# Expert layer of a decoder kernel: fp16 products from two scaled parts, and its sums spread over three engines

## The reference, cut to what matters

```python
x = x + self_attention_0(layernorm(x))
x = x + cross_attention_0(layernorm(x), ctx)
x = x + experts(layernorm(x))            # the part that changes
x = x + linear_attention_1(layernorm(x))
x = x + cross_attention_1(layernorm(x), ctx)
x = x + quantised_ffn(layernorm(x))

def experts(x, gate_w, weight):          # gate_w 8 x 256, weight 8 x 256 x 256
    logits = einsum('bsd,ed->bse', x, gate_w)
    topk_vals, topk_idx = top_k(logits, 2)
    topk_weights = softmax(topk_vals)
    one_hot = one_hot(topk_idx, 8)
    weights_full = einsum('bsk,bske->bse', topk_weights, one_hot)
    expert_out = einsum('bsd,edh->bseh', x, weight)
    return einsum('bse,bseh->bsh', weights_full, expert_out)
```

## Time and profile before

| what | us |
|---|---|
| median of 3 runs (2026.10 to 2026.39) | 2026.26 |
| the profiled execution | 2026.75 |
| its span | 2025.0 |
| TensorE busy (share of the span) | 1762.7 (87%) |
| VectorE busy | 1612.1 (80%) |
| ScalarE busy | 1334.7 (66%) |
| GpSimd busy | 274.6 (14%) |

### The profile page before, as it was taken

The page is one execution under the profiler, slowest core; times in us unless marked ns, Lnnn a source line. Parts: engine busy times, 40 slices in busy tenths (PEclk is TensorE's granted clock), DMA queues, the critical chain, the costliest instruction groups (busy, mean ns, idle before and its releaser), DMA issues. The chain is left out here.

```text
span 2025.0 us, 39718 instructions
## 1 busy us (share of the span) xinstructions
PE 1762.7 (87%) x14926; PEld 707.2 (35%) x14926; DVE 1612.1 (80%) x2323; ACT 1334.7 (66%) x2530; POOL 274.6 (14%) x534
## 2 busy tenths in 40 slices
PE   7757989999999999989999999997799775589962
PEld 3421222322332232223222222222444443367641
DVE  3789999989999999878999999990677676566656
ACT  3325989889889989978999999997210443234341
POOL 0810111211111021111101010100200132000003
PEclk9967999999999999989999999999899988699985
DMA  4000000000000001000000000000100000000001
GB/s 122 0 0 1 2 1 1 2 1 2 2 1 2 1 1 51 2 1 2 1 1 2 1 2 1 2 2 30 56 0 0 1 0 0 0 1 1 1 1 42
DMA packets 11147, 17.38 MB, mean 9 GB/s; under 512 B 1857, under 2 KB 9025, under 8 KB 10721
## 3 DMA queue, kind: packets, MB, share of 16 engines
q1 hardware_dynamic: 10128, 13.64, 2.1%
q10 hardware_dynamic: 848, 1.38, 0.2%
HBM read 12.92 MB, written 2.10 MB: 7 GB/s over the span
## 5 line engine op out<-in xcount | busy, mean ns | idle before, releaser
L968 DVE TENSOR_REDUCE mxp<-ps_m 128x2 f32<-128x1024 f32 (+1 forms) x960 | 1089.5, 1187 | 92.6 <-PE ps_m L779 91.0
L903 ACT ACTIVATE work<-ps_s 128x512 f32<-128x512 f32 x1856 | 1010.5, 598 | 135.1 <-PE ps_s L792 86.3
L806 PE MATMUL ps_av<-work,vst 128*32 128x256 f32 x7424 | 595.9, 393 | 11.9 <-ACT avs L910 11.2
L779 PE MATMUL ps_m<-k_stack,qa 48*128 48x512 f16 (+1 forms) x2048 | 380.2, 369 | 24.1 <-DVE mxp L968 23.5
L792 PE MATMUL ps_s<-qb,k_stack 50*128 50x512 f16 x1856 | 365.8, 383 | 31.0 <-ACT work L903 24.9
L806 PEld LDWEIGHTS ps_av<-work,vst 128*32 128x32 f32 x7424 | 147.4, 108 | 347.6 <-ACT work L903 259.5
L792 PEld LDWEIGHTS ps_s<-qb,k_stack 50*128 50x128 f16 x1856 | 109.5, 93 | 424.7 <-ACT work L903 408.6
L779 PEld LDWEIGHTS ps_m<-k_stack,qa 48*128 48x128 f16 x2048 | 105.5, 95 | 66.7 <-DVE mxp L968 56.3
L1175 PE MATMUL mprodp<-w_experts,mxt 128*128 128x512 f32 x256 | 117.2, 602 | 0.0
L198 PE MATMUL prod<-w_qkv,xt 128*128 128x512 f32 (+1 forms) x256 | 93.2, 508 | 7.1 <-DVE k_rows L1100 6.7
L1247 DVE SCALAR_TENSOR_TENSOR x_res<-mprodp,mmix,x_res 128x256 f32 (+1 forms) x128 | 61.7, 482 | 31.0 <-PE mprodp L1175 30.5
(11 more groups left out here) (309 smaller groups left out, 1783.9 us busy)
## 6 DMA issues: line engine op xcount, KB each, us to landing
x_res<-in_x SPq DMA_DIRECT2D x4, 512.0 KB, 13.6
w_experts<-in_w_experts SPq DMA_DIRECT2D x1, 2048.0 KB, 7.9
out<-x_res SPq DMA_DIRECT2D x8, 256.0 KB, 2.1
ctx_c<-in_ctx_c SPq DMA_DIRECT2D x1, 1664.0 KB, 8.4
work<-in_ctx_t SPq DMA_DIRECT2D x1, 784.0 KB, 11.2
w_qkv<-in_w_qkv ACTq DMA_DIRECT2D x1, 768.0 KB, 11.1
w_qkv<-in_w_qkv SPq DMA_DIRECT2D x1, 768.0 KB, 4.0
work<-in_ctx_t SPq DMA_DIRECT2D x1, 672.0 KB, 6.7
```

The source lines that it names most:

```text
L779: m = pe.matmul(ps_m[:, b, e, col:col + width], qa[n % 3][e * HALF:e * HALF + MAXROWS, j, a, :], STACKS[g][e * HALF:e * HALF + MAXROWS, gr ...
L806: m = pe.matmul(ps_av[32 * h:32 * h + 32, cols], vst[n % 2][:, t, h, :], pbuf[(tau[n] + t) % 2][:, h, cols], start=(t == 0 and half == 0), ...
L903: a.activation(pbuf[g % 2][:, h, :], ps_s[:, b, :], ACT.Exp, scale=factor).then_inc(s["exp"], 1)
L968: v.tensor_reduce(dst, src, AX.X, ALU.max).then_inc(s["mred"], 1)
```

## The change

What it does:

- **Weights.** The experts' weights, scaled by a power of two, are split into a high and a low fp16 part (`weh`, `wel`, together 32 KB of a partition, in the memory of the layer's first key stack, which now lives on). VectorE does it in the last attention unit: the peak at step 0, the rest behind two small products of TensorE at steps 5 and 7 that bring the peak to all partitions.
- **Rows.** A tile's turned rows times 64 are split too: ScalarE writes the high part `xh`, VectorE the low part `xl`. The float32 copy `xt` stays, for the gate. The gate's weights are divided by the scales (`gain`).
- **Products.** Each bank is six fp16 multiplications, high times high, high times low, low times high, in place of two in float32. The banks are filled in the order 3, 2, 0, 1.
- **Sums.** Bank 3, and bank 2 of the odd tiles, are weighed by ScalarE into SBUF (`scaled`), and GpSimd adds those parts to `x` after VectorE has added its own: two additions for even tiles, four for odd ones, each behind the last. VectorE is left with six or four. The statistics of a tile wait for GpSimd and stand one tile later on VectorE.
- **Fetch.** The normalising of the rows goes from VectorE to GpSimd.
- The loop is written out for all 16 tiles.

```diff
+ROW_GAIN = 64.0
...
+                    if expert_peak_at(n, t):
+                        pe.wait_ge(s["kpeak"], 4)
+                        b = take_m()
+                        pe.transpose(ps_m[0:1, b, 0, 0:P], wpeak[:, :], ident[:, :]).then_inc(s["mx"], 1)
+                    if expert_spread_at(n, t):
+                        pe.wait_ge(s["mred"], expert_peak_done)
+                        b = take_m()
+                        pe.matmul(ps_m[:, b, 0, 0:1], ones[0:1, :], wtop[:, :], start=True, stop=True).then_inc(s["mx"], 1)
...
+                    if (n, t) == (NCH - 1, 0):
+                        v.wait_ge(s["late"], 16 * len(later))
+                        v.tensor_reduce(wpeak[:, :], we[:, :, :], AX.XY, ALU.max, apply_absolute_value=True).then_inc(s["kpeak"], 1)
+                    if expert_peak_at(n, t):
+                        b = take()
+                        v.tensor_reduce(wtop[:, :], ps_m[0:1, b, 0, 0:P], AX.X, ALU.max).then_inc(s["mred"], 1)
+                    if expert_spread_at(n, t):
+                        b = take()
+                        v.tensor_copy(wbound[:, :], ps_m[:, b, 0, 0:1]).then_inc(s["mred"], 1)
+                        v.wait_ge(s["mred"], taken[0])
+                        cw = Counted(v, s["wchain"])
+                        power_scale(v, cw, wbound[:, :], wfloor[:, :], wscale[:, :], wback[:, :])
+                        cw(v.tensor_scalar(gain[:, :], wscale[:, :], ROW_GAIN, None, ALU.mult))
+                        cw(v.tensor_scalar(weh[:, :, :], we[:, :, :], wscale[:, :], None, ALU.mult))
+                        cw.wait()
+                        cw(v.scalar_tensor_tensor(wel[:, :, :], we[:, :, :], wscale[:, :], weh[:, :, :], ALU.mult, ALU.subtract))
+                        cw.wait()
...
-def experts(prog, x, st, mean, rstd, gate, w, iota, ident):
+def experts(prog, x, st, mean, rstd, gate, weh, wel, gain, iota, ident):
...
+    ORDER = (3, 2, 0, 1)
...
+    def by_act(n):
+        return (3,) if n % 2 == 0 else (3, 2)
+    def by_dve(n):
+        return [b for b in ORDER if b not in by_act(n)]
+    def more_until(n):
+        return sum(2 * len(by_act(m)) for m in range(n))
...
+        xh, xl = ([sb(f"mx{k}{p}", [P, 2, P], F16) for p in range(2)] for k in "hl")
+        scaled = [sb(f"mscaled{p}", [P, 4, D]) for p in range(2)]
...
+        @block.gpsimd
+        def _(g):
+            def fetch(n):
+                if n >= 2:
+                    g.wait_ge(s["turned"], n - 1)
+                g.tensor_scalar(xn[n % 2][:, :], x[:, n, :], mean[:, n:n + 1], rstd[:, n:n + 1], ALU.subtract, ALU.mult)\
+                 .then_inc(s["fetch"], 1)
+            fetch(0)
+            fetch(1)
+            for n in range(T):
+                if n + 2 < T:
+                    fetch(n + 2)
+                g.wait_ge(s_free[by_act(n)[-1]], n + 1)
+                g.wait_ge(s_free[by_dve(n)[-1]], n + 1)
+                done = more_until(n)
+                for i in range(2 * len(by_act(n))):
+                    if i > 0:
+                        g.wait_ge(s["more"], done)
+                    g.tensor_tensor(x[:, n, :], x[:, n, :], scaled[n % 2][:, i, :], ALU.add).then_inc(s["more"], 1)
+                    done += 1
...
+            def turn_tile(n):
+                pe.wait_ge(s["fetch"], n + 1)
+                if n >= 2:
+                    pe.wait_ge(s["low"], n - 1)
...
-            def multiply(n, p):
-                if has(n + 1):
-                    turn_tile(n + 1, 1 - p)
-                for b in range(4):
-                    if b == 1 and has(n + 1):
-                        logits(n + 1, 1 - p)
-                    s_used.wait(pe, 4 * n + b - 3)
-                    for k in range(2):
-                        m = pe.matmul(prod[:, b, :], xt[p][:, k, :], w[:, k, b * 512:b * 512 + 512],
-                                      start=(k == 0), stop=(k == 1))
-                    m.then_inc(s_w.sem, 1)
-            s_gate.open(pe)
...
+            def products(n, b):
+                if n >= 1:
+                    pe.wait_ge(s_free[b], n)
+                cols = slice(b * 512, b * 512 + 512)
+                for k in range(2):
+                    pe.matmul(prod[:, b, :], xh[n % 2][:, k, :], weh[:, k, cols], start=(k == 0), stop=False)
+                    pe.matmul(prod[:, b, :], xh[n % 2][:, k, :], wel[:, k, cols], start=False, stop=False)
+                for k in range(2):
+                    m = pe.matmul(prod[:, b, :], xl[n % 2][:, k, :], weh[:, k, cols], start=False, stop=(k == 1))
+                m.then_inc(s_prod[b], 1)
+            turn_tile(0)
+            logits(0)
+            for n in range(T):
+                if n + 1 < T:
+                    turn_tile(n + 1)
+                pe.wait_ge(s["low"], n + 1)
+                products(n, ORDER[0])
+                if n + 1 < T:
+                    logits(n + 1)
+                for b in ORDER[1:]:
+                    products(n, b)
...
-            def copy(n, p):
-                s_w.wait(a, 4 * (n - 1))
-                a.wait_ge(s_turned, n + 1)
-                a.copy(xt[p][:, :, :], turn[p][:, 0:D].rearrange("p (k n) -> p k n", k=2)).then_inc(s_copied.sem, 1)
-                a.wait_ge(s_d, n + 1)
-                a.activation(ex[:, :], dif[:, :], ACT.Exp).then_inc(s_e, 1)
...
+            def prepare(n):
+                a.wait_ge(s["turned"], n + 1)
+                if n >= 2:
+                    a.wait_ge(s["gate"], n - 1)
+                src = turn[n % 2][:, 0:D].rearrange("p (k n) -> p k n", k=2)
+                a.copy(xt[n % 2][:, :, :], src).then_inc(s["copied"], 1)
+                if n >= 2:
+                    a.wait_ge(s_prod[ORDER[-1]], n - 1)
+                a.activation(xh[n % 2][:, :, :], src, ACT.Copy, scale=ROW_GAIN).then_inc(s["high"], 1)
+            def exponent(n):
+                a.wait_ge(s["dif"], n + 1)
+                a.activation(ex[:, :], dif[:, :], ACT.Exp).then_inc(s["exp"], 1)
+            def weigh(n, i):
+                b = by_act(n)[i]
+                a.wait_ge(s["mix"], (n + 1) * per)
+                if n >= 2:
+                    a.wait_ge(s["more"], more_until(n - 1))
+                a.wait_ge(s_prod[b], n + 1)
+                for h in range(2):
+                    e = 2 * b + h
+                    m = a.activation(scaled[n % 2][:, 2 * i + h, :], half(b, h), ACT.Copy, scale=mix[n % 2][:, e:e + 1])
+                m.then_inc(s_free[b], 1)
+            prepare(0)
+            exponent(0)
+            for n in range(T):
+                if n + 1 < T:
+                    prepare(n + 1)
+                weigh(n, 0)
+                if n + 1 < T:
+                    exponent(n + 1)
+                if len(by_act(n)) > 1:
+                    weigh(n, 1)
...
+            def low(n):
+                v.wait_ge(s["high"], n + 1)
+                if n >= 2:
+                    v.wait_ge(s_prod[ORDER[-1]], n - 1)
+                v.scalar_tensor_tensor(xl[n % 2][:, :, :], turn[n % 2][:, 0:D].rearrange("p (k n) -> p k n", k=2), ROW_GAIN,
+                                       xh[n % 2][:, :, :], ALU.mult, ALU.subtract).then_inc(s["low"], 1)
+            def statistics(n):
+                v.wait_ge(s["more"], more_until(n + 1))
+                v.bn_stats(st[:, n, :], x[:, n, :]).then_inc(s["st"], 1)
...
+                v.wait_ge(s["exp"], n + 1)
+                c(v.tensor_scalar(den[:, :], ex[:, :], 1.0, gain[:, :], ALU.add, ALU.mult))
...
-            def body(n, p):
-                if has(n + 2):
-                    v.wait_ge(s_turned, n + 1)
-                    fetch(v, xn[p], n + 2).then_inc(s_fetch, 1)
...
+            def accumulate(n):
+                we = mix[n % 2]
+                c = Counted(v, s["sum"], sum(len(by_dve(m)) for m in range(n)))
+                for b in by_dve(n):
+                    v.wait_ge(s_prod[b], n + 1)
+                    c(v.scalar_tensor_tensor(x[:, n, :], half(b, 0), we[:, 2 * b:2 * b + 1], x[:, n, :], ALU.mult, ALU.add))
+                    yield
+                    c.wait()
+                    v.scalar_tensor_tensor(x[:, n, :], half(b, 1), we[:, 2 * b + 1:2 * b + 2], x[:, n, :], ALU.mult, ALU.add)\
+                     .then_inc(s_free[b], 1)
+                    yield
+                    v.wait_ge(s_free[b], n + 1)
+            low(0)
+            for _ in mixture(0):
+                pass
+            for n in range(T):
+                if n + 1 < T:
+                    low(n + 1)
+                turns = [accumulate(n)] + ([mixture(n + 1)] if n + 1 < T else [])
                 while turns:
                     turns = [g for g in turns if next(g, "done") != "done"]
-            for n in range(2):
-                fetch(v, xn[n], n).then_inc(s_fetch, 1)
-            list(mixture(0, 0))
-            every(body, v)
+                if n >= 1:
+                    statistics(n - 1)
+            statistics(T - 1)
...
+        ks = sb(ctx, "k_stack", [P, H // 2, S], F16)
```

(2 more changed lines are left out.)

109 lines of the change are left out of this document (40 added, 69 removed).

## The result

| kernel | median us | lowest to highest | runs |
|---|---|---|---|
| before | 2026.33 | 2026.10 to 2026.39 | 4 |
| changed | 2006.88 | 2006.14 to 2007.64 | 4 |

By the medians the changed kernel takes 19.5 us less, 0.9904 of the time before; the ratio estimated from all fast runs is 0.9898, 95% interval 0.9885 to 0.9912. The forecast was 2010. The median lies at the lower end of the range of 2006 to 2019, 0.9 us inside it; by the ratio the time is 2005.7, 0.3 us under it. The profiled execution took 2007.64 us.

What follows compares the result with a forecast made beforehand. TensorE's float32 product columns were taken to bound the expert stage; fp16 products with two late chains cut it from 126.1 to 109.6 us, 16.5 less, minus 0.3 for small matmuls: 16.2 less, about 2010 us, range 2006 to 2019.

Steps and rivals of the forecast that it cites:

- TensorE's bare tile: Expert stage: 5.20 us of fp16 products plus 0.66 of transposes and logits, 5.86 us a tile without waits.
- ScalarE's chain: Exponential, two bank 2 weighings, then copy: TensorE waits 0.7 us for the copy before every second tile's logits.
- E: The end of the odd tile's last product on TensorE, from which the times within a pair are counted.
- GpSimd's chain: Four additions of 0.83 us from E + 1.87, then a 1.22 us fetch, handed over at E + 6.46.
- GpSimd's slowness: Rival: beside busy VectorE, an add takes 1.05 us and a fetch 1.6; 2021 us, half of it 2015.5; chance 0.22.
- The pair: Odd tile and the even one behind it in the expert stage: 12.5 us in place of 15.08, eight times.
- Start and end of the stage: Expert stage's edges: 5.5 us as before, plus 0.8 for the first fetch and 3.3 for the last adds.
- The split: Attention's last unit: VectorE's weight split, high and low part 4.5 us each, done at 1405.5, covered with 4 us spare.
- Outside the stage: Two small TensorE matmuls in the attention's last unit were to cost 0.3 us.
- The likeliest case: The forecast itself: a pair between 12.2 and 12.9 us, 2007.5 to 2013.5 us; chance 0.60.
- rival C: TensorE's clock drops to 1.2 GHz in the stage through its new waits; 2052 us if half the products; chance 0.04.
- rival B: Both new waits vanish, a pair takes 2 x 5.86 = 11.7 us, 6 us less, 2004 us; chance 0.08.

Runs made afterwards that it cites:

- one_bank: Changed kernel with ScalarE weighing one bank in every tile instead of two in odd ones: 2000.26 us; repeated beside the changed kernel, 2000.23 us.
- weigh_first: Changed kernel with ScalarE weighing bank 2 of an odd tile before the next tile's exponential instead of behind it: 2002.80 us.
- early_fetch: Changed kernel with GpSimd's normalising fetch issued one tile earlier, ahead of a tile's additions instead of behind them: 2008.35 us.
- no_adds: Changed kernel with each GpSimd addition replaced by a copy of one column, so the output lacks what ScalarE weighed: 2006.66 us.
- weigh_early: Changed kernel with ScalarE weighing both banks before the exponential and GpSimd fetching three tiles ahead: 2003.38 us.
- split_thrice: Changed kernel with the high and low part of the weights computed three times in the same place: 2014.36 us.
- fp16_vector: Changed kernel's fp16 products, but all eight sums and the fetch on VectorE, nothing weighed by ScalarE, GpSimd idle: 1999.06 us; repeated, 2000.32 us.

## Why the prediction was right in kind, and which terms were off

The mechanism came as forecast: TensorE's products, now in fp16, bound the tile, and every second tile has a new wait for ScalarE's copy. What failed are sizes in the sum, all to the same side: the 5.86 us of TensorE's bare tile, which measured 5.76 (1.6 us in 16 tiles); the charge of this wait to eight pairs, while it occurs seven times (0.8 us); and the 0.3 us outside the stage, where the span gained 0.7.

**Products: right.** TensorE bounds the stage before, and its columns were the gain. 24 products of 0.217 apart were taken from another stage; the stage's own are 0.215 apart on average (six from 1506.68 to 1507.97 in the even tile of the timeline).

**TensorE's bare tile: 0.1 us too long.** I kept 0.66 us of the earlier trace rows for transposes and logits, worked out from a tile of float32 records. The trace of after has 5.76 where I had 5.86: 24 x 0.215 = 5.16 and 0.60. Over 16 tiles this is 1.6 us, the largest error of the sum.

**ScalarE's chain: right in kind, and placed to 0.1 us.** The exponential was to start at E + 0.77 and starts at E + 0.82; the copy was to be there at E + 2.13, and TensorE takes it at E + 2.07; the wait was to be 0.7 and is shown as 0.56, counted from the modelled end of the last product. Counted as the prediction counts it, from when TensorE could issue (in a tile without the wait the logits start 0.22 us behind the last product before them, which here would be 1505.49), it is 0.72. The next transposes come at E + 6.42, where I had TensorE ready at E + 6.42 and the fetch's handover at E + 6.46. That this chain, with the second bank in it, holds the pair, one_bank shows, and weigh_first for the most part of it.

**GpSimd's chain: its place right, its weight not.** The additions start at E + 1.84 (E + 1.87), take 3.21 (3.32), and the fetch lands at E + 6.26 (E + 6.41). I called both chains equal, and gave GpSimd's slowness 0.22 of the chance. The additions take 735 ns on average, so that rival is out, and early_fetch and no_adds show that GpSimd's chain has no share in the pair of this kernel. "Both chains end within 0.05 us of one another" was too close: the fetch has 0.16 us to spare in this order, and weigh_early shows it as the next limit. The Trainium skill, GPSIMD Engine Reference, section Engine selection, which the prediction weighed, says to keep elementwise work on VectorE. I read its factor of 2 as a price per addition; here it is 735 ns against the 484 of VectorE's weigh-and-add, 1.5. The kernel without the additions of GpSimd is the faster one all the same. In the loop that is not by their price: what costs there is ScalarE's share, without which GpSimd has nothing to add. At the end of the stage it is: no_adds, which shortens them alone, saves 2.3 us there.

**The pair** is 12.35 in place of 12.5. Two bare tiles are 11.52 of it, where I had 11.72, and the wait with what hangs on it adds 0.83, where I had 0.78. **The number of waits** is seven. I multiplied the pair by eight and so charged one wait that does not occur, 0.8 us. **Start and end of the stage** are what is left: 107.6 - 16 x 5.76 - 7 x 0.83 = 9.6 us, just as I had them, and the last statistics end 4.85 us behind the last product (4.9). Together: 1.6 and 0.8 too much, 7 x 0.05 = 0.35 too little, the stage is 2.0 us shorter than the 109.6 of the sum.

**The split: covered, with twice the cover.** I bounded the high part by 4.5 us from above and half of it from below, and took 4.5. It takes 2.34: the lower bound was the right one. Done at 1401.8 and not 1405.5, with 8.1 us to spare and not 4. This did not move the time, since either is covered, and split_thrice measures the cover. The two small products of TensorE are there, 0.27 and 0.38 us; I took 0.3 us for them, and the normalising is 0.35 later, but the experts start where they did, so no run shows that these 0.3 reach the time.

**Outside the stage** I had + 0.3; the rest of the span is 0.7 us shorter (19.2 - 18.5). From the last statistics to the first `ps_kv` product behind the experts both kernels take 20.1 us, and behind that one the changed kernel 427.9 in place of 428.7: the gain is in the later stages. Its cause stays open; kernels with the same code there take 427.7 to 429.2, so it may be none of the change's.

The sum was 16.2 us and the span gave 19.2: 2.0 of the stage and 1.0 outside it. The likeliest case's range allowed for a pair of 12.2 but not for the terms around it.

**The clock did not drop**: 1.00 from 1460 on, with a standstill of 0.56 us in seven pairs. So rival C was out. The Trainium skill, TensorE: Matmul & The Clock Gate, section A second HAM failure mode: psum-queue depth-cycling, tells of a loop that kept losing its clock by short waits; this loop does not.

**The step that I never took.** I followed three engines through the spread sums and did not ask what VectorE would need alone. The trace of the kernel before tells it, VectorE's busy time in the stage (third number behind the length):

```profile
1450.10:1576.20 126.10, 123.29 (x352) 59.47 (x352) 87.75 (x352) 13.03 (x35) 0.00 (x0) 0.98 0.00 0
```

87.75 us in 16 tiles are 5.5 a tile. With the low part, 0.41 as a SCALAR_TENSOR_TENSOR, it would need 5.9 against TensorE's 5.8: the spreading had at most some 0.1 us a tile to win (estimates, from these two busy times), and my own pair charged it 12.5 - 2 x 5.86 = 0.78 us every second tile and 3.3 at the end, 9.5 in all. Both numbers were there, and rival B even had the 2 x 5.86; I never laid them side by side. This would not have moved the forecast of this change, but it would have said which part of it to leave out. fp16_vector is the run for it: 5.6 us a tile on VectorE (77.6 of 80), 0.3 under the estimate, 5.76 on TensorE, 6 to 8 us less in all.
